# The last block's out-projection in a Mamba and mixture-of-experts layer: first half of the channels in the last scan steps, the rest behind the scan, the skip term added on TensorE

## The reference, cut to what matters

```python
h = h * dA + (delta_t * x_t)[..., None] * B_t[:, None, :]     # the scan, 1024 channels x 16 states
y_t = jnp.einsum('bdn,bn->bd', h, C_t)
...
y = y + xc * D_param            # the skip term
y = y * jax.nn.silu(z)          # the gate
return jnp.einsum('bld,ed->ble', y, out_proj_w)
```

## Time and profile before

| what | value |
|---|---|
| median of 3 runs | 2017.07 us (2016.44 to 2018.59) |
| profiled execution, its own time | 2018.3 us |
| its span | 2016.5 us |
| busy share of the span | PE 85%, PEld 62%, DVE 73%, ACT 40%, POOL 52% |
| mamba | up to about 1265 us of the span, then shared and experts |

### The profile page before, as it was taken

One profiled execution on the slowest core, in us unless ns is written; L12 is line 12 of the kernel. 1 busy time (PEld: TensorE's weight loads), 2 busy tenths in 40 slices (PEclk: granted clock), 3 DMA queues, 4 the chain that ended last, 5 costly groups with the idle time before them and its releaser, 6 DMA issues. The chain is left out here.

```text
span 2016.5 us, 28338 instructions
## 1 busy us (share of the span) xinstructions
PE 1707.2 (85%) x7908; PEld 1247.5 (62%) x7908; DVE 1481.7 (73%) x1981; ACT 804.5 (40%) x1190; POOL 1054.7 (52%) x823
## 2 busy tenths in 40 slices
PE   3857778598788888886867888999979999999998
PEld 2335444464445554445544454777869998999997
DVE  0379999999899999999999950567725566656564
ACT  0456556466566465564564421100012323323222
POOL 0069559787489595697886753000014443434343
PEclk9967988699898789996988879999989999999999
DMA  4212211222113222122222243211216665665664
GB/s 97 70 44 57 71 42 43 69 81 89 63 59 121 61 72 89 58 75 78 63 84 62 85 141 115 67 63 63 86 37 139 159 162 140 154 163 129 163 170 69
DMA packets 131940, 184.19 MB, mean 91 GB/s; under 512 B 23313, under 2 KB 81441, under 8 KB 128609
## 3 DMA queue, kind: packets, MB, share of 16 engines
q1 hardware_dynamic: 109200, 132.52, 20.6%
q0 software_dynamic: 17856, 44.85, 11.5%
q10 hardware_dynamic: 4720, 4.86, 0.9%
HBM read 277.64 MB, written 38.15 MB: 157 GB/s over the span
## 5 line engine op out<-in xcount | busy, mean ns | idle before, releaser
L1093 POOL TENSOR_TENSOR arena_kept<-arena_kept,b_all 128x512 f32<-128x512 f32 x512 | 638.0, 1277 | 251.1 <-DVE arena_kept L980 221.7
L980 DVE TENSOR_TENSOR_SCAN arena_kept<-da,arena_kept 128x512 f32<-128x512 f32 x512 | 597.7, 1205 | 36.8 <-ACT da L834 13.0
L631 PE MATMUL hT<-ident_kept,arena_kept 128*128 128x128 f32 x2048 | 329.7, 310 | 185.6 <-DVE yacc L998 111.9
L834 ACT ACTIVATE da<-arena_kept,a_neg 128x504 f32<-128x504 f32 x512 | 345.8, 684 | 318.4 <-DVE arena_kept L980 314.9
L631 PEld LDWEIGHTS hT<-ident_kept,arena_kept 128*128 128x128 f32 x2048 | 268.1, 159 | 298.7 <-DVE arena_kept L980 230.9
L998 DVE SCALAR_TENSOR_TENSOR yacc<-hT,c_now,yacc 128x512 f32<-128x512 f32 x480 | 333.4, 734 | 19.0 <-PE hT L631 17.9
L1997 POOL DMA_INDIRECT out<-y,slots_kept x76 | 132.1, 1738 | 268.5 <-issue 194.3
L478 PE MATMUL bank<-hid,wt 128*128 128x512 f32 x512 | 253.1, 643 | 6.4 <-ACT conv_sum L684 5.4
L478 PEld LDWEIGHTS bank<-hid,wt 128*128 128x128 f32 x512 | 102.4, 210 | 118.4 <-issue 109.4
L1633 POOL DMA_DIRECT2D slots_kept<-lists_kept x1 | 0.6, 568 | 252.2 <-DVE lists_kept L1583 252.2
L539 PE MATMUL bank<-skip,wt 128*128 128x512 f32 x256 | 126.7, 644 | 2.5 <-DVE skip L929 2.5
(11 more groups left out here) (218 smaller groups left out, 3181.6 us busy)
## 6 DMA issues: line engine op xcount, KB each, us to landing
w_up_kept<-in_up_T SPq DMA_DIRECT2D x76, 1408.0 KB, 6.1
w_dn_kept<-in_dn_T SPq DMA_DIRECT2D x76, 768.0 KB, 7.4
b_all<-bt_scratch SPq DMA_DIRECT2D x128, 256.0 KB, 3.6
wt<-in_in_T SPq DMA_DIRECT2D x64, 256.0 KB, 3.0
wt<-in_out_T SPq DMA_DIRECT2D x32, 256.0 KB, 3.0
x_in<-in_x_pad ACTq DMA_DIRECT2D x16, 256.0 KB
res<-in_x_pad SPq DMA_DIRECT2D x16, 256.0 KB, 4.1
x_scratch<-res SPq DMA_DIRECT2D x16, 256.0 KB, 2.0
```

The costliest lines, as they stand in the source:

```text
L631: mm = nc.tensor.transpose(turned_in(j, m, t)[:, d * P:(d + 1) * P], h[:, m % RING, d, t * P:(t + 1) * P], ident[:])
L834: nc.scalar.activation(out[:, :, 1:], rows[:, :, 1:], ACT.Exp, scale=a_neg[:, d, n:n + 1]) \
L980: nc.vector.tensor_tensor_scan(h[:, n % RING, i, :], da[i % RING][:], dbx[:, i, :], 0.0, ALU.mult, ALU.add).then_inc(scan_done, 1)
L1093: nc.gpsimd.tensor_tensor(dbx[:, i, :], u[:, d, :], b_all[:, m % RING, :], ALU.mult) \
```

## The change

In the last block alone, the out-projection of the first four channel tiles becomes four pieces pre0 to pre3 in steps 27 to 30 of the scan, with x1T taking their result. Behind the scan `last_turn` adds the skip term as a product with the identity in the same bank as the turned sums (which are now products too, since they accumulate), VectorE only gates, and post0 to post3 contract the other four channel tiles, each product waiting for its own tile's gate, and the residual; VectorE adds the result to x1T. The code of a switched-off variant (SHIFTED, an empty tuple) goes away. Cut to its core:

```diff
-     ["ct", "dt1"], ["ln1", "dt2", "w2"], ["ln2", "z5", "w3"], ["dt3", "z6", "row0"],
-     ["ln3", "z7", "row1"], ["row2", "row3", "zsilu1"], ["lg"], []],
+     ["ct", "dt1"], ["ln1", "dt2", "w2"], ["ln2", "z5", "w3"], ["dt3", "z6", "row0", "pre0"],
+     ["ln3", "z7", "row1", "pre1"], ["row2", "row3", "zsilu1", "pre2"], ["lg", "pre3"], []],
...
-AFTER = ["turn1"] + [f"out{i}" for i in range(2 * KM)] + ["xa"] + [
+AFTER = ["turn1"] + [f"post{f}" for f in range(KM)] + ["xa"] + [
...
+    if name == "pre":
+        return j == NBLK - 1
...
             load_res(NBLK)
+            for m in (STEPS, STEPS + 1):
+                for n in tiles_due(NBLK - 1, m):
+                    load_tile(n)
...
+            def last_turn(at):
+
+                pe.wait_ge(skip_ready, NBLK * DT + SKIP0)
+                for d in range(HT):
+                    bank = take(at, d)
+                    nc.tensor.matmul(bank[:], ident[:], skip[:, HT + d, :], start=True, stop=False)
+                    pe.wait_ge(sum_done, sums(NBLK - 1, STEPS - 1, TB - 1))
+                    for t in range(TB):
+                        mm = nc.tensor.matmul(bank[:, t * P:(t + 1) * P], yacc[:, t, d * P:(d + 1) * P], ident[:],
+                                              start=False, stop=(t == TB - 1))
                     mm.then_inc(bank_full, 1)
...
+            def pre_proj(section, j, at, f):
+
+                bank = take(at)
+                pe.wait_ge(y_ready[0], (at.block + 1) * HT + Y0)
+                w = tile_of(section, j, f"pre{f}")
+                for d in range(HT):
+                    mm = nc.tensor.matmul(bank[:], w[:, d, :], skip[:, d, :], start=(d == 0), stop=(d == HT - 1))
+                mm.then_inc(bank_full, 1)
+
+            def post_proj(section, j, at, f):
+
+                bank = take(at)
+                w = tile_of(section, j, f"post{f}")
+                for d in range(HT):
+                    pe.wait_ge(dve_emptied, Place(section, j, "turn1").dve + d + 1)
+                    nc.tensor.matmul(bank[:], w[:, d, :], skip[:, HT + d, :], start=(d == 0), stop=False)
+                pe.wait_ge(res_full, 16 * TB * at.block)
+                for t in range(TB):
+                    mm = nc.tensor.matmul(bank[:, t * P:(t + 1) * P], res[:, t, f * P:(f + 1) * P], ident[:],
+                                          start=False, stop=(t == TB - 1))
+                mm.then_inc(bank_full, 1)
...
+                elif name == "pre":
+                    x1_out(at, i)
...
+            def gate_last(at, i):
+
+                d = HT + i
+                if i == 0:
+                    dve.wait_ge(zs_ready, NBLK * HALVES)
+                dve.wait_ge(bank_full, at.full + i + 1)
+                nc.vector.tensor_tensor(skip[:, d, :], banks[at.uses[i].bank][:], zs[:, d, :], ALU.mult).then_inc(dve_emptied, 1)
+
+            def x1_rest(at, f):
+
+                dve.wait_ge(bank_full, at.full + 1)
+                dve.wait_ge(act_emptied, Place("body", NBLK - 1, f"pre{f}").act + 1)
+                nc.vector.tensor_tensor(x1T[:, f, :], banks[at.bank][:], x1T[:, f, :], ALU.add).then_inc(dve_emptied, 1)
...
-            pool.wait_ge(y_ready[1], NBLK * HT)
+            pool.wait_ge(dve_emptied, Place("after", NBLK, "turn1").dve + HT)
```

More of the change, by code:

```diff
@@ L68, in name_and_number @@
     return name, int(piece[len(name):] or 0)
-EMPTIED_BY_ACT = {"cond", "x", "rank", "bc", "dt", "z", "out", "xr", "w", "row", "lg"}
-EMPTIED_BY_DVE = {"turn", "ct", "xa"}
+EMPTIED_BY_ACT = {"cond", "x", "rank", "bc", "dt", "z", "out", "pre", "xr", "w", "row", "lg"}
+EMPTIED_BY_DVE = {"turn", "ct", "post", "xa"}
 EMPTIED = EMPTIED_BY_ACT | EMPTIED_BY_DVE
@@ L158, in __init__, with sums @@
                 self.dve = use.place
[L161 to L183, removed]
+def sums(j, m, t):
+    return (j * STEPS + m) * TB + t + 1
 def turned_bc(block):
     return Place("ahead", 0, "ct") if block == 0 else Place("body", block - 1, "ct")
-STREAMED = {"x", "z", "out", "xa", "w"}
+STREAMED = {"x", "z", "out", "pre", "post", "xa", "w"}
 STREAM = [(section, j, piece) for section, j, pieces in SECTIONS for piece in pieces
@@ L369, in load_tile @@
                     tile = out_wT[:, i % 2 * HT:i % 2 * HT + HT, i // 2 * P:(i // 2 + 1) * P]
+                elif name in ("pre", "post"):
+                    tile = out_wT[:, (HT if name == "post" else 0):(DT if name == "post" else HT), i * P:(i + 1) * P]
                 elif name == "xa":
@@ L520, in turn @@
             def turn(at, half):
-                pe.wait_ge(sum_done, sums_by_dve(at.block - 1, STEPS - 1, TB - 1) if half else sums_by_dve(at.block, NST - 1, TB - 1))
+                pe.wait_ge(sum_done, sums(at.block - 1, STEPS - 1, TB - 1) if half else sums(at.block, NST - 1, TB - 1))
                 for d in range(HT):
@@ L546, in out_proj, with x1_made @@
                     mm.then_inc(bank_full, 1)
+            def pre_proj(section, j, at, f):
[15 more added lines that the diff above has]
+                                          start=False, stop=(t == TB - 1))
+                mm.then_inc(bank_full, 1)
+            def x1_made(section, j):
+                if section == "after":
+                    pe.wait_ge(dve_emptied, Place(section, j, f"post{KM - 1}").dve + 1)
+                else:
+                    pe.wait_ge(act_emptied, Place(section, j, f"out{2 * KM - 1}").act + 1)
             def x1_row(section, j, at, t):
                 bank = take(at)
-                pe.wait_ge(act_emptied, Place(section, j, f"out{2 * KM - 1}").act + 1)
+                x1_made(section, j)
                 for k in range(KM):
@@ L603, in piece_of @@
                     dt_proj(section, j, at, i)
+                elif name == "turn" and section == "after":
+                    last_turn(at)
                 elif name == "turn":
@@ L625, in turn_h @@
                         of, step, tile = at // SUMS, at % SUMS // TB, at % TB
[L626 to L629, removed]
+                        pe.wait_ge(sum_done, sums(of, step, tile))
                     for d in range(HT):
@@ L1094, in inflow @@
                     .then_inc(dbx_made, 1)
-            def add_shifted(j, m, t):
-                pool.wait_ge(scaled[t], scaled_by_act(j, m))
-                nc.gpsimd.dma_start(out=yacc[:, t, :], in_=stage[:, SHIFTED.index(t), :], accum_op=ALU.add) \
-                    .then_inc(added[t], ADDED)
             pool.wait_ge(itok_in, 16)
@@ L1115, in _ @@
                         inflow(j, *divmod(m, NST), i)
-                    for t in SHIFTED:
-                        if m >= 2 and (m - 2) % NST and shifted(m - 2, t):
-                            add_shifted(j, m - 2, t)
                     for behind, name in ((1, "gate"), (2, "ln")):
```

40 lines of the change are left out of this document (10 added, 30 removed).

## The result

The changed kernel took 2003.82 us (median of 4 runs, 2003.51 to 2005.72), the kernel before 2017.58 (4 runs): ratio 0.9931, 95% interval 0.9919 to 0.9944, 13.8 us less. 2005.8 was forecast, so 11.3 less.

A forecast was written before the change was run, and what follows sets the result against it. Bound: the 41.2 us from VectorE's last sum to the adapters' matmul, mostly TensorE alone. Gain 14.5 behind, less 3.2 ahead, is 11.3: 2018.3 to 2007.0, less 1.2 above the median, 2005.8 us; range 2001.5 to 2011.5.

The forecast's parts named there:

- Behind S, the count: From S, the end of VectorE's last sum, to the adapters' matmul: 24.5 us at full clock instead of 41.2.
- The clock: ... I take the 2.2 measured at this place: Slow clock at the start of TensorE's work behind the last sum: 2.2 us, bounds nothing to 6.2.
- pre3 ... It hides, with 1.0 us to spare: Step 30: pre3 runs 1180.7 to 1184.2, the fourth turned tile to 1184.6, its sum due at 1185.6.
- rival 2: pre3 at half clock takes 6.9 us, last sum +7.7, turning starts at full clock: 9.0 us gained, 2008.1; chance 0.20.
- The hand order on TensorE, steps 27 to 29: Added half-projections delay step 28's sums by 1.9 us and the scans of steps 30 and 31 by 3.2 and 3.8.
- Transposes into products: Last turning: a tile's eight product instructions take 0.89 us, four of a transpose 0.44, a factor of two.
- Beside POOL: VectorE's new adds beside POOL's weight splits: 0.69 us taken for the last add, bounds 0.69 to 3.43.
- POOL and SP: Later loads of B cost nothing, 2.6 us of cover; POOL's splits end about 1232, 20 us of cover.
- rival 5: Splits or stores bound the next part, so an earlier x1 buys nothing: 2017 us; chance 0.02.
- rivals 1, 3 and 4: S +0.5, 2000.9 us (0.12); S +10, no tellable change, 2016.6 (0.06); half clock from step 27, slower, 2041.6 (0.04).

The follow-up runs named there:

- after: The changed kernel itself, unedited, first trace, against the kernel before: 2003.82 us, ratio 0.9931.
- mixed: Changed kernel with two last tiles' skip term on TensorE, laid ahead of the last sum's wait, two with transposes and VectorE's add and gate: 2001.31 us.
- skip_on_vector: Changed kernel with the skip term back on VectorE, turned tiles as transposes, gate waits still tile by tile: 2003.06 us.
- pre_light: Changed kernel with each half-projection contracting one channel tile instead of four; copies, loads and waits stay: 2004.87 us, one run.
- skip_only: Changed kernel with no half-projection moved ahead of the last sum; skip term on TensorE and waits tile by tile stay: 2014.52 us.

## Why the prediction was right

The forecast of 2005.8 us was 2.0 too high: 11.3 us net of the change's own terms, where the traces have 12.45 three times. Two of its steps were off, by 2.1 us behind S and by 0.95 ahead of it, in opposite directions, and they are named below. Of the 13.8 us between the medians 1.3 belong to neither term; in the two later pairs of medians that rest is 1.1 and 0.0.

**Behind S, the count: right to 0.1 us.** The 24.5 us at the full clock (6.2 turning, 17.3 in four groups, 1.0 to the adapters) were measured as 6.31, 17.31 and 0.99, together 24.61, in three traces out of three.

**"The clock: ... I take the 2.2 measured at this place": mis-sized, 0 measured.** The granted clock was 1.00 from 1184 on. It had fallen earlier, as the stretches of after show (columns as in the earlier trace rows):

```profile
1172.00:1174.00 2.00, 2.00 (x21) 2.00 (x19) 2.00 (x4) 1.99 (x2) 2.00 (x3) 1.00 0.30 95
1174.00:1176.00 2.00, 2.00 (x17) 2.00 (x17) 0.49 (x1) 1.97 (x4) 2.00 (x3) 0.82 0.94 303
1176.00:1178.00 2.00, 2.00 (x11) 2.00 (x11) 1.34 (x2) 1.40 (x4) 0.60 (x2) 0.50 0.99 318
...
1182.00:1184.00 2.00, 2.00 (x6) 0.74 (x5) 1.19 (x2) 0.00 (x0) 0.00 (x0) 0.97 0.00 0
1184.00:1188.00 4.00, 3.56 (x23) 2.31 (x21) 3.38 (x5) 0.59 (x1) 0.00 (x0) 1.00 0.63 199
```

**"pre3 ... It hides, with 1.0 us to spare": failed in all three traces of the changed kernel, by the clock.** TensorE in steps 29 and 30 of after:

```profile
1168.46 3.63 PE L550 MATMUL bank<-skip,wt 128*128 128x512 f32 x8
...
1172.36 4.17 PE L610 MATMUL bank<-gate_T,x2T 128*128 128x16 f32 x32
1176.36 2.80 PE L659 MATMUL hT<-ident_kept,arena_kept 128*128 128x128 f32 x12
1178.96 5.17 PE L550 MATMUL bank<-skip,wt 128*128 128x512 f32 x8
1183.97 2.82 PE L659 MATMUL hT<-ident_kept,arena_kept 128*128 128x128 f32 x20
```

The logits came in 4.17 us, under the 5 asked for, but the clock fell while TensorE was at them, to 1.2 GHz (0.50), and came back some 3 us into pre3. The three turned tiles and pre3 behind them took 2.60 and 5.01 us from start to start, where mixed, at 1.00, has 1.34 and 3.43; the fourth turned tile was 1.42 us late for its sum. So S moved by 4.15 and not 3.2. With the clock at 1.00 through the same stretch (mixed, skip_on_vector) the same program up to S needs 37.2 instead of 38.7, which puts 1.5 us on the clock and leaves 2.65 for the load; there pre3 does hide. So the 3.2 was 0.55 too high for the full clock that it was worked out for, and the slow spell, which it had left to rival 2, put 1.5 on top.

**Rival 2 came half true.** It had the clock fall within the logits and the turning start at the full clock, both seen; but it had pre3 at half speed throughout, 6.9 us and S at +7.7. The prediction charged one slow spell, 2.2 us, behind S; in after it came ahead of S, where it cost 1.5. That the net still came near, 16.6 - 4.15 = 12.45 us by the trace against 14.5 - 3.2 = 11.3, is in part luck. Where a slow spell falls, and whether one falls at all, no run here lets one forecast: skip_on_vector paid 2.28 behind S and nothing ahead of it, and mixed, at 1.00 throughout, paid nothing in either place.

**The hand order on TensorE, steps 27 to 29: right.** Sums of step 28 at +1.94 (+1.9 forecast), scan of step 30 at +3.1 (+3.2), scan of step 31 at +3.6 (+3.8), all counted from step 28. Behind the scan of step 31 the forecast took 0.6 back for the wait that goes; at full clock (mixed, whose scan of step 31 is at +3.6 as well) 0.95 came back. That TensorE's load and not ScalarE's copy sets these was assumed there; pre_light shows it (0.13 left without the load).

**Transposes into products.** In skip_only the eight instructions of a tile's four products go from 1192.85 to 1193.74, 0.89 us (in mixed two tiles take 1187.34 to 1189.25, 0.95 each with the start), where four transposes take 0.44 at the full clock: the factor of two taken. "TensorE: Matmul & The Clock Gate" of the Trainium skill, section Terms, has four for FP32; the rows do not agree with it. The prediction's working from it, a gain about 1 us smaller, does not follow either: it keeps the products at 0.89 and makes the transposes shorter, and neither the 6.2, built from the products' row, nor the turning before, paced by VectorE, depends on these.

**Beside POOL: right where taken, and with one neighbour overlooked.** x1_rest took 0.69 us each beside POOL's splits, the lower bound. But VectorE's own split of the first x2, never named in the prediction, now also lies beside them. VectorE in after:

```profile
1207.48 0.69 DVE L955 TENSOR_TENSOR x1T<-bank,x1T 128x512 f32<-128x512 f32 x1 [3.63 <-PE bank L562]
...
1217.01 2.93 DVE L1197 CAST x_hi_kept<-arena_kept 128x2048 fp32r<-128x2048 f32 x1
1219.98 3.72 DVE L1201 TENSOR_TENSOR x_lo_kept<-arena_kept,x_hi_kept 128x2048 fp32r<-128x2048 f32 x1
```

and the same two in the kernel before, where POOL's splits had ended at 1227.3:

```profile
1231.44 1.22 DVE L1185 CAST x_hi_kept<-arena_kept 128x2048 fp32r<-128x2048 f32 x1
1232.69 2.29 DVE L1189 TENSOR_TENSOR x_lo_kept<-arena_kept,x_hi_kept 128x2048 fp32r<-128x2048 f32 x1
```

POOL's last split but one, beside them, took 5.37 us where such a split takes 3.43; the last one followed it:

```profile
1228.60 3.44 POOL L1201 TENSOR_TENSOR sdn_lo_kept<-hid,sdn_hi_kept 128x1536 fp32r<-128x1536 f32 x1
```

It costs nothing here: VectorE is done at 1223.7 and POOL at 1232.0, 29 and 20.5 us ahead of the shared part's first matmul.

**POOL and SP: right.** POOL waited for B in all three steps; the last such wait, in after:

```profile
1171.10 4.96 POOL L1114 TENSOR_TENSOR arena_kept<-arena_kept,b_all 128x512 f32<-128x512 f32 x4 [3.02 <-DMA b_all<-bt_scratch]
```

Its first tile is done at 1171.10 + 1.24 = 1172.3, 4.3 us ahead of the scan that uses it (2.6 forecast). Splits that end at 1232.0 (1232 forecast) and a first shared matmul at 1252.58 (1255 forecast, 2 of the 2.4 us from what precedes step 28) rule out rival 5; rivals 1, 3 and 4 fall with S, which moved by 4.15 us and not by 0.5, 10 or 39.

## What to carry to other kernels

Work moved under a full engine is not hidden but paid at the exchange rate of that engine's spare time in each step. Here 13.8 us of TensorE's work (4 x 8 x 0.43) made the last sum 2.7 us late with the clock at full, and 3.9 to 4.15 with a slow spell in it; with two of the four pieces in emptier steps it was 2.0, and 1.5 in one more trace. So the table should be filled where the engine has gaps and not where the result is due. Behind a scan, where one engine is alone, give small sums to the idle one: the skip term wholly on TensorE cost some two us more than on VectorE, and half on each (mixed) was the best found, though its lead in the medians is small. And a slow spell of the clock is to be given a range and not one value, with the question where it may fall and who waits there: here it cost 0 to 2.3 us.

## What the runs showed of the hardware that was not expected

- **Where the clock falls differs between kernels that are the same up to that place.** Three traces of the unedited kernel had it fall between 1174 and 1177, within or just behind the logits; skip_on_vector, whose program differs only behind S, kept 1.00 from 1136 to about 1189 and fell there, and mixed, also different only behind S, held 1.00 from 1136 to 1230. Already between 1100 and 1132 their granted clocks differ. Whether it is the run or the program that decides this was not settled, as each of these two has one trace; it is worth 1.5 to 2.3 us here.
- **A cast on VectorE beside POOL's splits took 2.93 us in after and 4.10 in mixed, where it took 1.22.** "SBUF — State Buffer" of the Trainium skill, section Who interferes with whom, says that a cast can take the port pair that VectorE shares with GpSimd, and that the later of the two then waits for the whole of the other's instruction; the rows agree. The cast began 1.84 us (after) and 3.01 us (mixed) ahead of the end of the POOL split under way, and took 1.71 and 2.88 us longer than alone. The sums with one operand in PSUM kept their 0.69.
